# Queries of batches 1 to 3 from high and low parts of weights and rows, in three single-pass products

## The chip, the cores and the metric

The kernel runs on one core of a Trainium2 chip. The metric is the time of one execution on the device in microseconds, as the median of several runs. One execution was also taken with the hardware profiler; its rows are what the prediction reads.

## The reference, cut to what matters

The reference is one layer of a gated cross-attention block with a mixture of experts behind it, for 4 batches of 512 rows of 512 numbers. Only the first step matters here:

```
q = layernorm(x) @ w_q.T        # 4 x 512 x 512, 32 heads of 16
k = ctx @ w_k.T                 # 8 groups of 16
v = ctx @ w_v.T
scores = q k^T / 4, causal, masked; softmax; times v; out @ w_o.T + b_o
x = x + tanh(g_xattn) * that    # then the experts on layernorm(x)
```

Queries and keys are wanted in float32 accuracy, since the scores feed an exponential.

## The kernel before, in words

The program is a chain of stages with a barrier between two of them: `stage_project`, `stage_attend`, `stage_close`, `stage_shared`, `stage_experts`. The change lies in `stage_project` (line 242), which lasts from 0 to about 115 us. It goes through four batches, one block of code per engine, and the engines meet by semaphores.

TensorE (lines 455 to 527): for batch b it turns the four 128-row chunks of the normalised rows (`turn`, line 474, four 128x128 transposes each into one of two PSUM banks `tps`), with the keys of the batch (`keys`, line 458) behind the second turn and the values (`values`, line 466) behind the fourth. In batch 0 keys and values stand first. Then come the queries (`queries`, line 493): four output groups i of 128 query columns, each into its own PSUM bank `proj[i]` and each made of four products, over the four 128-row slices k of the weights `wq`, against the turned rows `xnT` of 512 columns. Both are float32, and the profiler records two instructions for each such product. In the last batch `scores` (line 483) puts one pair of score products of the first two rounds behind each of the sixteen query products. A pair goes into two of three banks, and `max_pair` (line 201) first waits until VectorE has taken the maxima of the pair before: all but the last of them, or, for one pair in a round of eight, all of them (line 204). One transpose of the maxima (`turn_maxima`, line 214) follows the tenth pair.

ScalarE (lines 410 to 453) copies PSUM to SBUF in this order per batch: two turned chunks, the keys' high part, two more turned chunks, the values, the root for the next batch's layernorm (`deviation`), and then the high part of each query group as it comes. A high part is the copy in the type float32r, which holds fewer bits and goes through TensorE in a single pass; the low part is what is left, PSUM minus high part.

VectorE (lines 368 to 408) makes the low part of the keys, then the layernorm of the next batch (`normalise`), then the low parts of the four query groups; in the last batch also the maxima of the score pairs, four pairs ahead of each low part.

GpSimd (lines 321 to 366) fills constants and then stores the keys' parts of each batch to DRAM. SP issues all loads, then the stores of the queries' parts in order of the batches (`store_q`, line 284), and behind those of batch 1 the loads of the first three rounds of scores (line 317).

The buffers `parts[0]` and `parts[1]` hold the high and low parts of a batch in turns; batch 0 and 2 use the first, 1 and 3 the second. Fillers of TensorE (48 bf16 products, line 527) close the stage.

For comparison, `stage_shared` (line 1438) and `stage_experts` (line 1729) already multiply in three float32r products, high by high, high by low and low by high.

Of the kernel before, what the change touches and what calls it, by code (L numbers as in the profile page):

```python
# [16 lines left out]
P = 128  # L17
# [78 lines left out]
def begin(eng, *made):  # L96

    for sem in made:
        eng.sem_inc(sem, 1)  # L99
# [142 lines left out]
def stage_project(nc, io, dram):  # L242

    SPIN, SEAM = 48, 48
    with ExitStack() as c:  # L245
# [2 lines left out]
        sem = dsem = lambda n: c.enter_context(nc.semaphore(n))  # L248

        parts = [sb(f"p_parts{i}", [P, KD + 1, 2, SEQ], F32R) for i in range(2)]  # L250
        wq, wk, wv = sb("wq", [P, KD, D]), sb("wk", [P, KD, P]), sb("wv", [P, KD, P])
        x, ctx = [residual(io, b) for b in range(BATCH)], [context(io, b) for b in range(BATCH)]
        xn, xnT = sb("p_xn", [P, CH, D]), sb("p_xnT", [P, KD, SEQ])
        stats, mv, rstd = sb("p_stats", [P, CH, 6]), sb("p_mv", [P, CH, 2]), sb("p_rstd", [P, CH])
        root, work, eps = sb("p_root", [P, CH]), sb("p_work", [P, CH]), sb("p_eps", [P, 1])
        v = io["v_all"]
        ident = io["ident"]
        padi, padb = sb("p_padi", [BATCH, SEQ], I32), sb("p_padb", [BATCH, SEQ], F32R)
        padf = sb("p_padf", [BATCH, SEQ])
# [8 lines left out]
        s_kmm, s_vmm, s_qmm = sem("p_skmm"), sem("p_svmm"), sem("p_sqmm")  # L268
        s_khi, s_klo, s_qhi, s_qlo, s_vcp = (sem(f"p_s{n}") for n in ("khi", "klo", "qhi", "qlo", "vcp"))
        s_fill, s_mask, s_warm = (sem(f"p_s{n}") for n in ("fill", "mask", "warm"))  # L270
        s_one = dsem("p_sone")
        s_pad, s_padb, s_padf, s_pout = dsem("p_spad"), sem("p_spadb"), sem("p_spadf"), dsem("p_spout")
        s_qout, s_kout = io["s_qout"], io["s_kout"]
# [2 lines left out]
        @block.sync  # L276
        def _(eng):
            def load_ctx(b):
                eng.dma_start(ctx[b], io["ctxT"][:, b * SEQ:(b + 1) * SEQ].rearrange("(c p) n -> p c n", p=P)).then_inc(s_ctx[b], 16)

            def load_x(b):
                eng.dma_start(x[b], io["x"][b * SEQ:(b + 1) * SEQ, :].rearrange("(j p) d -> p j d", p=P)).then_inc(s_x[b], 16)

            def store_q(b):
                for i in range(KD):
                    at = dram["q"][b * GROUPS + 2 * i:b * GROUPS + 2 * i + 2].rearrange("g t r s j n -> s (g t r) (j n)")
                    eng.wait_ge(s_qhi, b * KD + i + 2)
# [9 lines left out]
            eng.dma_start(padi[:], io["mask"]).then_inc(s_pad, 16)  # L297
            load_x(0)
            eng.dma_start(wv[:], io["wvT"].rearrange("(c p) n -> p c n", p=P)).then_inc(s_wv, 16)
            eng.dma_start(wq[:], io["wqT"].rearrange("(c p) n -> p c n", p=P)).then_inc(s_wq, 16)  # L300
            for b in range(1, BATCH):
                load_x(b)
                load_ctx(b)
            eng.wait_ge(s_padb, 2)
            for b in range(BATCH):
                eng.dma_start(dram["k"][b * GROUPS:(b + 1) * GROUPS, ROW_PAD].rearrange("(o g) n -> o g n", o=1),
                              padb[b:b + 1, :].bitcast(F32).rearrange("p (o n) -> p o n", o=1).broadcast_to([1, GROUPS, SEQ])).then_inc(s_pout, 16)
            for b in range(BATCH):
                store_q(b)
                if b == 1:  # L310
                    eng.wait_ge(s_pout, 16 * BATCH)
                    eng.wait_ge(s_one, 64 * NB)
                    eng.wait_ge(s_qout[0], 16 * 2 * KD)
                    eng.wait_ge(s_kout[0], 48)
                    eng.wait_ge(s_vcp, 2)
                    for i in range(NB - 1):
                        load_scores(eng, io, dram, i, i)
                    for i in range(NB - 1):
                        load_values(eng, io, i, i)

        @block.gpsimd
        def _(eng):
            begin(eng, s_eps, s_ones, s_fill, s_mask, s_warm)
            eng.memset(io["onesb"], 1.0).then_inc(s_warm, 1)
            eng.memset(io["before"], 1.0).then_inc(s_fill, 1)
            eng.memset(io["ident"], 0.0).then_inc(s_fill, 1)
# [32 lines left out]
                    eng.dma_start(k[r][HALF * t + ROW_MAX:HALF * t + ROW_MAX + 1].bitcast(F32), const[:, 1]).then_inc(s_one, 16)  # L359
            for b in range(BATCH):  # L360
                at = dram["k"][b * GROUPS:(b + 1) * GROUPS]
                eng.wait_ge(s_khi, b + 2)
                for slot in range(2):
                    eng.dma_start(at[:, slot:2 * HD:2], parts[b % 2][:, KD, 0].bitcast(F32)).then_inc(s_kout[b % 2], 16)
                eng.wait_ge(s_klo, b + 2)
                eng.dma_start(at[:, 2 * HD:3 * HD], parts[b % 2][:, KD, 1].bitcast(F32)).then_inc(s_kout[b % 2], 16)

        @block.vector
        def _(eng):
            begin(eng, s_newton, s_st, s_mv, s_xn, s_klo, s_qlo, s_padb, s_padf, io["s_rmax"], io["s_mr"])  # L370
            def normalise(b):
                eng.wait_ge(s_x[b], 16)
                for j in range(CH):
# [12 lines left out]
            eng.tensor_copy(padf[:], padi[:]).then_inc(s_padf, 1)  # L386
            eng.wait_ge(s_padf, 2)
            eng.tensor_scalar(padb[:], padf[:], 0.0, NEG, ALU.is_equal, ALU.mult).then_inc(s_padb, 1)
            def low_keys(b):
                eng.wait_ge(s_khi, b + 2)  # L390
                part = parts[b % 2][:, KD]
                eng.tensor_tensor(part[:, 1, :], proj[KD][:], part[:, 0, :].bitcast(F32), ALU.subtract).then_inc(s_klo, 1)

            normalise(0)
            for b in range(BATCH):
                low_keys(b)
                if b + 1 < BATCH:
                    normalise(b + 1)
                for i in range(KD):
                    if b == BATCH - 1:  # L400
                        for n in range(i * KD, (i + 1) * KD):
                            round, turn, j = n // (2 * CH), n // 2 % CH, n % 2
                            maxima(eng, io, round, round, turn, j)
                            if n == 2 * CH + 1:
                                take_row(eng, io, 0, 0)
                    part = parts[b % 2][:, i]
                    eng.wait_ge(s_qhi, b * KD + i + 2)
                    eng.tensor_tensor(part[:, 1, :], proj[i][:], part[:, 0, :].bitcast(F32), ALU.subtract).then_inc(s_qlo, 1)

        @block.scalar  # L410
        def _(eng):
            begin(eng, s_root, s_xT, s_khi, s_qhi, s_vcp)
            def deviation(b):
                eng.wait_ge(s_mv, (b + 1) * CH + 1)
                eng.activation(root[:], mv[:, :, 1], ACT.Sqrt, bias=eps[:]).then_inc(s_root, 1)

            def take_turned(b, j):
                eng.wait_ge(s_tr, b * CH + j + 2)
                eng.activation(xnT[:, :, j * P:(j + 1) * P], tps[j % 2], ACT.Copy).then_inc(s_xT, 1)

            def take_keys(b):
                eng.wait_ge(s_kmm, b + 2)
                if b >= 2:
                    eng.wait_ge(s_kout[b % 2], 48)
# [10 lines left out]
            for b in range(BATCH):  # L435
# [20 lines left out]
        def _(eng):  # L456
# [36 lines left out]
            def queries(b):  # L493
                eng.wait_ge(s_xT, (b + 1) * CH + 1)
                if b:
                    eng.wait_ge(s_qlo, b * KD + 1)
                for i in range(KD):
                    for k in range(KD):
                        mm = eng.matmul(proj[i][:], wq[:, k, i * P:(i + 1) * P], xnT[:, k, :], start=k == 0, stop=k == KD - 1)
                        if k == KD - 1:  # L500
# [1354 lines left out]
```

## Time and profile before

| | |
|---|---|
| runs | 1211.01 us median of 3 (1208.92 to 1211.45) |
| the profiled execution | 1205.16 us |
| its span, first to last instruction | 1203.4 us |
| mean granted TensorE clock | 0.990 of full speed |
| busy: TensorE, VectorE, ScalarE, GpSimd | 1163.3, 614.1, 563.9, 650.2 us |

The profiled execution is 5.85 us shorter than the runs' median and 1.76 us longer than its span. A granted clock of 1.00 is 2.4 GHz. PE is TensorE, PEld its weight loads, DVE is VectorE, ACT is ScalarE, POOL is GpSimd, SP issues transfers. `Lnnn` is a line of the kernel. Busy time of PE is modelled: its records of one float32 product overlap, so distances between starts say more than durations.

### The profile page before, as it was taken

Reading aid. Unit: us, or ns where it says so; the run is one execution under the profiler, and the core shown is the slowest. Engines: PE = TensorE matmul, PEld = TensorE weight load, DVE = VectorE, ACT = ScalarE, POOL = GpSimd, SP = SyncE. Lnnn points to the kernel's source line nnn. Section 1 sums busy time; section 2 is a strip of 40 time slices with the busy share of each in tenths; the row PEclk is TensorE's granted clock in tenths of the full one; section 3 lists DMA queues with packets and bytes.
Section 4 is the critical chain, followed back from the end, with each engine's and each line's share of the span. In section 5 each row is a group of like instructions: output and inputs, shape, how many; then the busy total and the mean of one; then the engine's idle time right before and its main releaser. Section 6 shows DMA issues by size and latency. Waiting matters only on the chain. (4 is left out here: it accounts for less than half of the span.)

```text
span 1203.4 us, 23285 instructions
## 1 busy us (share of the span) xinstructions
PE 1163.3 (97%) x7651; PEld 899.5 (75%) x7652; DVE 614.1 (51%) x1785; ACT 563.9 (47%) x981; POOL 650.2 (54%) x697
## 2 busy tenths in 40 slices
PE   7999999999997989999998999999999999999996
PEld 5564555555543468888877999999999999999995
DVE  5337999999966958721344033333423444442100
ACT  2221777777751333323222554554554554554552
POOL 5010333334342615788863666666767666676663
PEclk9999999999998999999998999999999999999998
DMA  9462544444449350120313655666666666566443
GB/s 347 176 189 96 156 128 127 127 126 130 133 143 238 137 213 33 38 65 12 138 56 116 144 118 110 143 150 149 142 150 150 144 150 148 144 150 149 74 69 42
DMA packets 77309, 157.95 MB, mean 131 GB/s; under 512 B 12933, under 2 KB 18821, under 8 KB 76217
## 3 DMA queue, kind: packets, MB, share of 16 engines
q1 hardware_dynamic: 54152, 107.12, 27.7%
q0 software_dynamic: 23088, 49.94, 21.7%
q8 instruction: 40, 0.66, 0.2%
q14 instruction: 29, 0.23, 0.1%
HBM read 101.97 MB, written 52.64 MB: 128 GB/s over the span
## 5 line engine op out<-in xcount | busy, mean ns | idle before, releaser
L1589 DVE CAST e_w<-e_w 128x480 fp32r<-128x480 f32 x135 | 80.5, 596 | 300.7 <-DMA e_w<-in_w2T 296.5
L670 DVE CUSTOM_DVE_ANT_0 a_mb<-a_mb,late 128x512 f32<-128x512 f32 (+1 forms) x480 | 217.4, 530 | 6.2 <-PE a_mb L714 4.6
L1750 PE MATMUL e_yps<-e_w,e_hT 128*128 x711 | 190.3, 394 | 0.9 <-ACT e_hT L1656 0.9
L576 POOL TENSOR_SCALAR_AFFINE_SELECT a_at<-a_at 128x256 f32<-128x256 f32 (+1 forms) x192 | 94.2, 491 | 171.0 <-ACT a_at L656 170.9
L656 ACT ACTIVATE a_at<-a_eb 128x1024 f32<-128x1024 f32 (+1 forms) x192 | 163.5, 870 | 38.3 <-PE a_eb L735 25.8
L1729 PE MATMUL e_up<-e_w,e_xT 128*128 x948 | 170.5, 329 | 0.0
L1729 PE MATMUL e_gate<-e_w,e_xT 128*128 x948 | 167.8, 326 | 0.5 <-issue 0.5
L1616 POOL DMA_INDIRECT out<-e_y,scatter x79 | 128.3, 1624 | 69.0 <-ACT e_y L1665 59.7
L1729 PEld LDWEIGHTS e_gate<-e_w,e_xT 128*128 128x128 f32 x948 | 158.8, 191 | 7.6 <-issue 0.9
L1750 PEld LDWEIGHTS e_yps<-e_w,e_hT 128*128 128x128 f32 x711 | 131.7, 189 | 25.6 <-issue 1.2
L1729 PEld LDWEIGHTS e_up<-e_w,e_xT 128*128 128x128 f32 x948 | 149.9, 189 | 0.0
L714 PE MATMUL a_mb<-a_k,a_q 49*128 49x512 f32 (+1 forms) x480 | 132.6, 373 | 0.8 <-PEq L245 0.8
L714 PEld LDWEIGHTS a_mb<-a_k,a_q 49*128 49x128 f32 x480 | 74.3, 184 | 65.6 <-DVE a_mx L670 39.3
L1634 POOL TENSOR_TENSOR e_h<-e_act,e_upc 128x352 f32<-128x352 f32 x79 | 76.8, 972 | 70.0 <-ACT e_upc L1678 69.9
L1621 POOL TENSOR_TENSOR e_hT<-e_hc,e_hT 128x384 fp32r<-128x384 f32 x78 | 87.0, 1115 | 41.0 <-ACT e_hc L1658 40.9
L758 PE MATMUL a_pv<-a_at,a_v 128*32 128x128 f32 (+1 forms) x1792 | 102.3, 327 | 0.5 <-POOL a_at L576 0.4
L1596 DVE TENSOR_TENSOR e_w<-e_w 128x480 fp32r<-128x480 f32 x135 | 96.8, 717 | 4.7
L1652 ACT ACTIVATE e_xT<-e_xps 128x512 fp32r<-128x512 f32 x79 | 47.2, 597 | 90.3 <-PE e_xps L1720 90.3
L105 POOL DMA_INDIRECT e_x<-dx,gather x79 | 80.7, 1021 | 13.8 <-issue 3.7
L735 PE MATMUL a_eb<-a_q,a_k 50*128 50x512 f32 (+1 forms) x256 | 84.2, 420 | 0.1
L1672 ACT ACTIVATE e_act<-e_gate 128x352 f32<-128x352 f32 x79 | 36.7, 465 | 93.0 <-PE e_gate L1729 93.0
L1387 POOL DMA_INDIRECT dtable<-r_put,r_place x64 | 66.2, 1034 | 17.3 <-issue 17.3
(256 smaller groups left out, 1783.1 us busy)
## 6 DMA issues: line engine op xcount, KB each, us to landing
e_w<-in_w13T SPq DMA_DIRECT2D x16, 1408.0 KB
dq<-p_parts SPq DMA_DIRECT2D x32, 256.0 KB, 2.4
a_q<-dq SPq DMA_DIRECT2D x64, 128.0 KB
do<-a_o SPq DMA_DIRECT2D x32, 256.0 KB, 2.3
e_w<-in_w2T SPq DMA_DIRECT2D x16, 512.0 KB
a_k<-dk SPq DMA_DIRECT2D x64, 98.0 KB
e_w<-in_ctxT SPq DMA_DIRECT2D x4, 1024.0 KB, 15.2
e_w<-in_x SPq DMA_DIRECT2D x4, 1024.0 KB, 13.6
```

The lines of the kernel that those rows point to most:

```text
L105: eng.indirect_dma_start(out=io["rows"][n], out_offset=None, in_=dram["x2"], in_offset=bass.IndirectOffsetOnAxis(ap=io["gather"][:, g:g + ...
L576: eng.affine_select(out=square, in_=square, compare_op=ALU.is_ge, fill=0.0, base=0, pattern=[[0, 2 * len(js)], [1, P]], channel_multiplier ...
L656: eng.activation(to, scores, ACT.Exp, scale=0.25).then_inc(s_exp, 1)
L670: eng.tensor_tensor_reduce(out=b[:, 0:w], in0=b[:, 0:w], in1=io["late"][:, SEQ - w:SEQ], scale=1.0, scalar=3 * NEG, op0=ALU.add, op1=ALU.m ...
L714: mm = eng.matmul(b, q[r][rows, j, ch * P:(ch + 1) * P], k[r][rows, 0:b.shape[-1]], start=True, stop=True)
L735: return eng.matmul(eb[u % 2][:, t, n0:SEQ], keys, q[r][rows, js[0], n0:SEQ], start=True, stop=True)
L758: mm = eng.matmul(pv[32 * h:32 * h + 32, cols], v[of % NB][:, ch, :], at[of % 2][:, ch, 2 * j + t, cols], start=ch == 0 and n0 == 0, stop= ...
L1596: eng.tensor_tensor(w[rows, r, rest], w[rows, r, rest].bitcast(F32), w[rows, r, cols].bitcast(F32), ALU.subtract).then_inc(s_low, 1)
L1616: eng.indirect_dma_start(out=out, out_offset=bass.IndirectOffsetOnAxis(ap=io["scatter"][:, g:g + 1], axis=0), in_=y[n][:], in_offset=None, ...
L1621: eng.tensor_tensor(hT[r][:, 1], hc[:], hT[r][:, 0].bitcast(F32), ALU.subtract).then_inc(s_hlow, 1)
L1729: mm = eng.matmul(out[r][:], xT[r][:, mine, k, :], w[:, bass.ds(buf, 1), its * SIDE + at:its * SIDE + at + INTER].rearrange("p b n -> p (b ...
L1750: mm = eng.matmul(yps[:], hT[r][0:size, mine, n, :], w[0:size, bass.ds(buf, 1), its * SIDE + at:its * SIDE + at + D].rearrange("p b n -> p ...
```

## The change

Batch 0 stays as it is, in float32; only its turned rows go into another buffer (`first`). For batches 1 to 3 each query group becomes twelve float32r products instead of four float32 ones: high weights by high rows, low weights by high rows, high weights by low rows. The high rows are ScalarE's copy as before, now in float32r. The low rows are four new VectorE subtractions per batch (`low_turned`), two ahead of the low keys and two behind them. The high weights are one new ScalarE copy in batch 0, and the low weights four new GpSimd subtractions ahead of batch 1's key stores. A turn into a bank now waits for the low rows made from it, and the queries of batches 1 to 3 wait for the low rows of their batch and for the low weights. In the last batch a score pair stands behind every third product, which makes sixteen as before. To make room, the float32 weights and batch 0's turned rows lie in the second parts buffer, and the mask's rows too; ScalarE's take of batch 1's keys therefore waits until the mask's rows are stored.

```diff
-        wq, wk, wv = sb("wq", [P, KD, D]), sb("wk", [P, KD, P]), sb("wv", [P, KD, P])
+        wlow, wk, wv = sb("p_wlow", [P, KD, D], F32R), sb("wk", [P, KD, P]), sb("wv", [P, KD, P])
+        wq, first = parts[1][:, KD // 2:KD].bitcast(F32).rearrange(...), parts[1][:, 0:KD // 2].bitcast(F32).rearrange(...)
-        xn, xnT = sb("p_xn", [P, CH, D]), sb("p_xnT", [P, KD, SEQ])
+        xn, xnT = sb("p_xn", [P, CH, D]), sb("p_xnT", [P, KD, SEQ], F32R)
+        xlow, whigh = sb("p_xlow", [P, KD, SEQ], F32R), sb("p_whigh", [P, KD, D], F32R)
-        padi, padb = sb("p_padi", [BATCH, SEQ], I32), sb("p_padb", [BATCH, SEQ], F32R)
-        padf = sb("p_padf", [BATCH, SEQ])
+        padi, padf, padb = xn[0:BATCH, 0].bitcast(I32), parts[1][0:BATCH, KD, 0].bitcast(F32), parts[1][0:BATCH, KD, 1]
...
 # GpSimd, in front of the stores of a batch's keys
+                if b == 1:
+                    eng.wait_ge(s_whigh, 2)
+                    eng.wait_ge(s_qmm, KD + 1)
+                    for k in range(KD):
+                        eng.tensor_tensor(wlow[:, k], wq[:, k], whigh[:, k].bitcast(F32), ALU.subtract).then_inc(s_wlow, 1)
...
 # VectorE
+            def low_turned(b, j):
+                columns = slice(j * P, (j + 1) * P)
+                eng.wait_ge(s_xT, b * CH + j + 2)
+                eng.tensor_tensor(xlow[:, :, columns], tps[j % 2], xnT[:, :, columns].bitcast(F32), ALU.subtract).then_inc(s_xlow, 1)
...
+                if b:
+                    low_turned(b, 0)
+                    low_turned(b, 1)
                 low_keys(b)
+                if b:
+                    low_turned(b, 2)
+                    low_turned(b, 3)
...
 # ScalarE
-                eng.activation(xnT[:, :, j * P:(j + 1) * P], tps[j % 2], ACT.Copy).then_inc(s_xT, 1)
+                eng.activation((xnT if b else first)[:, :, j * P:(j + 1) * P], tps[j % 2], ACT.Copy).then_inc(s_xT, 1)
...
+                if b == 1:
+                    eng.wait_ge(s_pout, 16 * BATCH)
                 eng.activation(parts[b % 2][:, KD, 0, :], proj[KD][:], ACT.Copy).then_inc(s_khi, 1)
...
+                if b == 0:
+                    eng.wait_ge(s_wq, 16)
+                    eng.activation(whigh[:], wq, ACT.Copy).then_inc(s_whigh, 1)
...
 # TensorE, in turn(b, j)
+                if t >= CH + 2:
+                    eng.wait_ge(s_xlow, t - CH)
 # and in queries(b)
+                if b:
+                    eng.wait_ge(s_whigh, 2)
+                    eng.wait_ge(s_wlow, KD + 1)
+                    eng.wait_ge(s_xlow, b * CH + 1)
                 for i in range(KD):
-                    for k in range(KD):
-                        mm = eng.matmul(proj[i][:], wq[:, k, i * P:(i + 1) * P], xnT[:, k, :], start=k == 0, stop=k == KD - 1)
...
+                    for n, (weights, rows, k) in enumerate((weights, rows, k) for weights, rows in ((whigh, xnT), (wlow, xnT), (whigh, xlow)) for k in range(KD)):
+                        mm = eng.matmul(proj[i][:], weights[:, k, columns], rows[:, k, :], start=n == 0, stop=n == 3 * KD - 1)
+                        if n == 3 * KD - 1:
                             mm.then_inc(s_qmm, 1)
-                        if b == BATCH - 1:
-                            scores(i * KD + k)
+                        if b == BATCH - 1 and n % 3 == 2:
+                            scores(i * KD + n // 3)
```

## Rows read from the trace of the kernel before

**Rows 1.** The page, busy time, share of the span, instructions.
```profile
PE 1163.3 (97%) x7651; PEld 899.5 (75%) x7652; DVE 614.1 (51%) x1785; ACT 563.9 (47%) x981; POOL 650.2 (54%) x697
```
**Rows 2.** Windows: stretch, length, busy (count) per engine, PEclk, DMA share, GB/s.
```profile
0.00:112.00 112.00, 104.77 (x433) 57.29 (x434) 55.95 (x198) 24.02 (x45) 23.23 (x47) 1.00 0.61 207
```
**Rows 3.** Timeline of TensorE, batch 1: start, duration, line, operation, count.
```profile
35.57 3.60 PE L463 MATMUL p_proj<-e_w,wk 128*128 128x512 f32 x8
39.00 1.04 PE L480 MATMUL a_mb<-ident,p_xn 128*128 128x128 f32 x8
...
43.45 13.90 PE L499 MATMUL p_proj<-p_xnT,wq 128*128 128x512 f32 x32
57.18 1.04 PE L480 MATMUL a_mb<-ident,p_xn 128*128 128x128 f32 x8
```
**Rows 4.** TensorE's timeline in the shared expert, and its loads by line (min/median/max ns).
```profile
498.98 2.88 PE L1438 MATMUL s_up<-s_xT,s_ws 128*128 x12
501.70 1.52 PE L1438 MATMUL s_gate<-s_xT,s_ws 128*128 x6
...
L1438 PEld LDWEIGHTS s_gate<-s_xT,s_ws x288: 186/188/189, 447.3 to 612.2; 128*128 128x128 f32 x144
```
**Rows 5.** Timeline of TensorE, batch 3: score pairs (L210) and query products.
```profile
90.87 0.49 PE L210 MATMUL a_mb<-a_k,a_q 49*128 49x256 f32 x2
91.29 1.12 PE L499 MATMUL p_proj<-p_xnT,wq 128*128 128x512 f32 x2
92.35 0.44 PE L210 MATMUL a_mb<-a_k,a_q 49*128 49x256 f32 x2
...
93.77 0.45 PE L210 MATMUL a_mb<-a_k,a_q 49*128 49x256 f32 x2
```
**Rows 6.** Timeline of VectorE, batch 3, a pair's maxima; in brackets idle time and releaser.
```profile
91.28 0.30 DVE L225 CUSTOM_DVE_ANT_0 a_mb<-a_mb,late 128x128 f32<-128x128 f32 x1 [0.47 <-PE a_mb L210]
...
92.15 0.14 DVE L225 DVE_READ_ACCUMULATOR2_ANT a_mx<- 128x1 f32 x1
```
**Rows 7.** Timeline of all engines at the end of the stage.
```profile
112.96 0.69 DVE L408 TENSOR_TENSOR p_parts<-p_proj,p_parts 128x512 fp32r<-128x512 f32 x1
...
115.58 0.33 SPq L175 DMA_DIRECT2D a_q<-dq  x1
```
**Rows 8.** Groups by form, ScalarE, 0 to 130 us: busy, mean ns, idle before.
```profile
L656 ACT ACTIVATE a_at<-a_eb 128x1024 f32<-128x1024 f32 x5 | 5.0, 1014 | 2.4 <-PE a_eb L734 1.3 <-PE a_eb L735 1.1
```
**Rows 9.** Timeline of ScalarE, batches 0 and 1.
```profile
22.29 0.30 ACT L415 ACTIVATE p_root<-p_mv,p_eps 128x4 f32<-128x4 f32 x1 [1.55 <-DVE p_mv L377]
24.59 0.60 ACT L453 ACTIVATE p_parts<-p_proj 128x512 fp32r<-128x512 f32 x1 [2.00 <-PE p_proj L499]
...
39.20 0.60 ACT L425 ACTIVATE p_parts<-p_proj 128x512 fp32r<-128x512 f32 x1 [2.73 <-PE p_proj L463]
```
**Rows 10.** One line's instructions, GpSimd in the experts: min/median/max ns.
```profile
L1621 POOL TENSOR_TENSOR e_hT<-e_hc,e_hT x78: 1002/1011/1571, 652.4 to 1186.4; 128x384 fp32r<-128x384 f32 x78
```
**Rows 11.** Timeline of GpSimd, the key stores of batch 1.
```profile
40.09 1.19 POOL L364 DMA_DIRECT2D dk<-p_parts  x2 [19.73 <-ACT p_parts L425]
```
**Rows 12.** Groups by form, VectorE, 0 to 113 us.
```profile
L408 DVE TENSOR_TENSOR p_parts<-p_proj,p_parts 128x512 fp32r<-128x512 f32 x16 | 11.0, 689 | 21.1 <-ACT p_parts L453 21.1
```
**Rows 13.** Timeline of VectorE, around batch 1.
```profile
35.52 0.69 DVE L408 TENSOR_TENSOR p_parts<-p_proj,p_parts 128x512 fp32r<-128x512 f32 x1 [2.74 <-ACT p_parts L453]
39.83 0.69 DVE L392 TENSOR_TENSOR p_parts<-p_proj,p_parts 128x512 fp32r<-128x512 f32 x1 [3.62 <-ACT p_parts L425]
...
48.71 0.68 DVE L408 TENSOR_TENSOR p_parts<-p_proj,p_parts 128x512 fp32r<-128x512 f32 x1
```
**Rows 14.** Windows, one microsecond, all engines.
```profile
39.00:40.00 1.00, 1.00 (x11) 1.00 (x10) 0.17 (x1) 0.80 (x2) 0.00 (x0) 1.00 0.00 0
```
**Rows 15.** Windows before and in a stretch of low granted clock.
```profile
636.00:639.00 3.00, 0.00 (x0) 0.00 (x0) 0.00 (x0) 0.00 (x0) 0.18 (x2) 1.00 0.16 61
...
642.00:645.00 3.00, 3.00 (x11) 3.00 (x11) 0.00 (x0) 0.00 (x0) 0.00 (x0) 0.50 1.04 403
```

More of the change, by code:

```diff
@@ L250, in stage_project @@
         parts = [sb(f"p_parts{i}", [P, KD + 1, 2, SEQ], F32R) for i in range(2)]
-        wq, wk, wv = sb("wq", [P, KD, D]), sb("wk", [P, KD, P]), sb("wv", [P, KD, P])
+        wlow, wk, wv = sb("p_wlow", [P, KD, D], F32R), sb("wk", [P, KD, P]), sb("wv", [P, KD, P])
+        wq, first = parts[1][:, KD // 2:KD].bitcast(F32).rearrange("p i t n -> p (i t) n"), parts[1][:, 0:KD // 2].bitcast(F32).rearrange("p i t n -> p (i t) n")
         x, ctx = [residual(io, b) for b in range(BATCH)], [context(io, b) for b in range(BATCH)]
-        xn, xnT = sb("p_xn", [P, CH, D]), sb("p_xnT", [P, KD, SEQ])
+        xn, xnT = sb("p_xn", [P, CH, D]), sb("p_xnT", [P, KD, SEQ], F32R)
+        xlow, whigh = sb("p_xlow", [P, KD, SEQ], F32R), sb("p_whigh", [P, KD, D], F32R)
         stats, mv, rstd = sb("p_stats", [P, CH, 6]), sb("p_mv", [P, CH, 2]), sb("p_rstd", [P, CH])
@@ L270, in stage_project @@
         s_fill, s_mask, s_warm = (sem(f"p_s{n}") for n in ("fill", "mask", "warm"))
+        s_xlow, s_whigh, s_wlow = sem("p_sxlow"), sem("p_swhigh"), sem("p_swlow")
         s_one = dsem("p_sone")
@@ L296, in _ @@
             load_ctx(0)
-            eng.dma_start(padi[:], io["mask"]).then_inc(s_pad, 16)
+            eng.dma_start(padi, io["mask"]).then_inc(s_pad, 16)
             load_x(0)
             eng.dma_start(wv[:], io["wvT"].rearrange("(c p) n -> p c n", p=P)).then_inc(s_wv, 16)
-            eng.dma_start(wq[:], io["wqT"].rearrange("(c p) n -> p c n", p=P)).then_inc(s_wq, 16)
+            eng.dma_start(wq, io["wqT"].rearrange("(c p) n -> p c n", p=P)).then_inc(s_wq, 16)
             for b in range(1, BATCH):
@@ L322, in _ @@
         def _(eng):
-            begin(eng, s_eps, s_ones, s_fill, s_mask, s_warm)
+            begin(eng, s_eps, s_ones, s_fill, s_mask, s_warm, s_wlow)
             eng.memset(io["onesb"], 1.0).then_inc(s_warm, 1)
@@ L369, in _ @@
         def _(eng):
-            begin(eng, s_newton, s_st, s_mv, s_xn, s_klo, s_qlo, s_padb, s_padf, io["s_rmax"], io["s_mr"])
+            begin(eng, s_newton, s_st, s_mv, s_xn, s_klo, s_qlo, s_padb, s_padf, s_xlow, io["s_rmax"], io["s_mr"])
             def normalise(b):
@@ L385, in _ @@
             eng.wait_ge(s_pad, 16)
-            eng.tensor_copy(padf[:], padi[:]).then_inc(s_padf, 1)
+            eng.tensor_copy(padf, padi).then_inc(s_padf, 1)
             eng.wait_ge(s_padf, 2)
-            eng.tensor_scalar(padb[:], padf[:], 0.0, NEG, ALU.is_equal, ALU.mult).then_inc(s_padb, 1)
+            eng.tensor_scalar(padb, padf, 0.0, NEG, ALU.is_equal, ALU.mult).then_inc(s_padb, 1)
             def low_keys(b):
@@ L411, in _ @@
         def _(eng):
-            begin(eng, s_root, s_xT, s_khi, s_qhi, s_vcp)
+            begin(eng, s_root, s_xT, s_khi, s_qhi, s_vcp, s_whigh)
             def deviation(b):
@@ L496, in queries @@
                     eng.wait_ge(s_qlo, b * KD + 1)
+                if b:
+                    eng.wait_ge(s_whigh, 2)
+                    eng.wait_ge(s_wlow, KD + 1)
+                    eng.wait_ge(s_xlow, b * CH + 1)
                 for i in range(KD):
-                    for k in range(KD):
-                        mm = eng.matmul(proj[i][:], wq[:, k, i * P:(i + 1) * P], xnT[:, k, :], start=k == 0, stop=k == KD - 1)
-                        if k == KD - 1:
+                    columns = slice(i * P, (i + 1) * P)
+                    if b == 0:
+                        for k in range(KD):
+                            mm = eng.matmul(proj[i][:], wq[:, k, columns], first[:, k, :], start=k == 0, stop=k == KD - 1)
+                        mm.then_inc(s_qmm, 1)
+                        continue
+                    for n, (weights, rows, k) in enumerate((weights, rows, k) for weights, rows in ((whigh, xnT), (wlow, xnT), (whigh, xlow)) for k in range(KD)):
+                        mm = eng.matmul(proj[i][:], weights[:, k, columns], rows[:, k, :], start=n == 0, stop=n == 3 * KD - 1)
+                        if n == 3 * KD - 1:
                             mm.then_inc(s_qmm, 1)
-                        if b == BATCH - 1:
-                            scores(i * KD + k)
+                        if b == BATCH - 1 and n % 3 == 2:
+                            scores(i * KD + n // 3)
             eng.wait_ge(s_warm, 3)
```

## The prediction

> **What bounds the kernel now.** I read the page first: TensorE is busy for 97% of the span [rows 1]. The page's chain of waits lies in the last half of the span, where the change does nothing, so I cut the span at 112 us, where the projections end. There TensorE is busy 104.77 of 112 us at a granted clock of 1.00, 2.4 GHz, VectorE 55.95 [rows 2]. The timeline of TensorE then shows no idle time between its pieces in batch 1: two turns and the keys, two turns and the values, then the queries, 32 records from 43.45 to 57.18 us, where batch 2's first turn starts [rows 3]. Batch 2 repeats the pattern. So a microsecond less of query products there is a microsecond less of the span, as long as no operand is late. Batch 3 is different: its query products stand between pairs of score products, and VectorE has to clear the banks of these [rows 5].
>
> **The products of batches 1 and 2.** They go from 16 float32 products to 48 float32r ones per batch. A float32 product is two records, 13.73 / 32 = 0.429 us apart, 0.858 us in all [rows 3]. Float32r products of the same form, 128x128 weights against 512 columns, run in the shared expert: a group of 12 from 498.98 to 501.70 us, 0.2267 us each [rows 4]. The price of a new batch is 48 x 0.2267 = 10.88 us, and 13.73 - 10.88 = 2.85 us are saved, 5.70 in two batches. The ends of this price: the float32 records at half their distance, 0.2145 us (10.30, saving 3.43), and the rival of exposed loads below.
>
> The Trainium skill (TensorE: Matmul & The Clock Gate, Back-to-back issue gap) gives an isolated product N/2.4 + 2.5 ns, 215.7 ns for 512 columns. By it a batch would take 10.35 us, and the whole change would give some 1.6 us more; the row above is slower, and I go by it.
>
> **Batch 3.** From one score pair to the next is 1.48 us (90.87 to 92.35) or 1.42 (92.35 to 93.77) [rows 5]. In the first of these the pair takes 0.42 us until a query product starts (91.29). That product's two records take 1.06 us, up to 92.35, where two in the stream take 0.858. I read the 0.20 as two weight loads of 0.10 that aren't hidden where pairs of 49 rows and products of 128 rows follow each other [rows 5]. With three float32r products between pairs 1.06 us becomes 3 x 0.227 + 2 x 0.10 = 0.88, and 0.18 us are saved per pair, at 1.30 and 1.25 us. Can VectorE keep that? It takes 0.87 us for a pair (91.28 to the second read at 92.15 [rows 6]) and 0.69 for the low part behind each fourth pair: 4 x 0.87 + 0.69 = 4.2 us against 4 x 1.28 = 5.1. It can. But one pair in eight (the third of a round) waits for both maxima of the pair before, and these end 92.15 + 0.14 - 90.87 = 1.42 us after that pair began, where TensorE would be there after 1.30; with the semaphore I take 1.47, so 0.17 is lost in the first round. In the second the turn of the maxima stands there and covers it. The first pair waits for ScalarE's copy of the values and gains 0.09 only. Sum: 15 x 0.178 + 0.09 - 0.17 = 2.6 us. Bounds: 0, if the pairs keep their pace, and 16 x 0.18 = 2.9. I take 2.6, since in the rows VectorE idles 0.47 us before a pair, waiting for TensorE [rows 6].
>
> The end of the stage stays as it is: behind the last pair come two maxima, the low part at 112.96, its store, and the next stage's first transfer at 115.58 [rows 7].
>
> **What is added, and what hides it.**
> The high weights, one ScalarE copy of 2048 columns: at 1014 ns for 1024 [rows 8] at most 2.03 us. It stands behind the root of 22.29 to 22.59 and ends by 24.6; the next ScalarE work began at 24.59 [rows 9]. Should it be late, only batch 0's first high part moves, and the next is due 3.4 us later. Cost 0.
>
> The low weights, four GpSimd subtractions of 512 columns. They wait for batch 0's last query product, whose low part VectorE made at 35.52 [rows 13], say for 35 us, and must be done before batch 1's queries at 43.45 [rows 3]. The nearest row is 1.011 us for 384 columns, 1.571 at its longest [rows 10]; by columns 1.35, at most 2.1. So 5.4 us, to 40.4; at the longest 8.4 us, to 43.4. Both are in time: cost 0, and beyond 2.1 us each, four times the excess. Behind them on GpSimd stand the stores of batch 1's keys, issued at 40.09 until now [rows 11]; they move by about 1 us. Their readers are SP's loads of scores of later rounds and the reuse of the buffer in batch 3, 40 us on.
>
> The low turned rows, four VectorE subtractions per batch of 0.69 us, the price of the like row [rows 12]. Two come before the low keys, while TensorE makes keys (35.57 to 39.00): the low part at 35.52 goes first [rows 13], then 36.2 to 37.6, and the turn at 39.00 that now needs the first of them has 2 us to spare. Two follow the low keys at 39.83 and end near 41.9, before the queries at 43.45. The normalising behind them starts 1.4 us later; its end, where batch 1's first low part starts at 48.71 [rows 13], becomes 50.1, and batch 2's turns need it at 43.45 + 10.88 = 54.3. Cost 0, with 1.5 us of cover; were that gone, a late microsecond would cost one in each of three batches.
>
> The mask's rows lie in the second parts buffer now, so ScalarE's take of batch 1's keys at 39.20 waits for their stores. Between 39 and 40 us no DMA moved anything [rows 9, 14], so they had landed. Cost 0. SP keeps its order; its stores follow the high and low parts, and the loads of scores behind batch 1's stores go out earlier with them.
>
> **Sum.** 5.7 + 2.6 = 8.3 us. What follows is started by semaphores and moves as a whole. The profiled execution is 1205.16 us for a span of 1203.4 and would be 1196.9. The runs' median, 1211.01, lies 5.9 above the profiled one, a difference of executions; the same 8.3 off it gives 1202.7.
>
> **Rivals.**
> *Weight loads show, and it is slower.* A batch loads 48 sets of weights where it loaded 32, in the same rows of the array. If each product showed the 0.10 us that batch 3's changes show, it would cost 0.327, a batch 15.7 us, 2.0 more than before, and batch 3's three products and pair load 1.08 for 1.06. In all 4 us slower, 1215. It decides from 13.73 / 48 = 0.286 us per product on. Against it: in the shared expert a load of 0.188 us stands behind each product and the distance is still 0.227 [rows 4]; for it, only batch 3, where the shapes alternate. The chance is 5%; a compiled form that isn't single-pass would end here too, another 1%.
> The Trainium skill (TensorE: Matmul & The Clock Gate, Part 3, The mechanism) says that a weight load overlaps running products only where the row group differs, and so speaks for this rival. This trace disagrees in [rows 4].
>
> *Batch 3 keeps its pace.* The pairs stay at 1.45 us because the banks' waits set them. Then 5.7 us are saved: 1205.3. For it: a wait on the maxima is at every pair. Against it: VectorE's idle time. 17%.
>
> *The low weights are late.* GpSimd at 3 us each would end at 47, 3.5 us late: 4.8 saved, 1206.2. At 4.2 each the gain is gone. Against it: the longest row. 8%.
>
> *The clock takes it back.* Behind stretches where TensorE stood the granted clock falls to 0.50, 1.2 GHz, for some microseconds: it did nothing from 636 to 639 us and runs at half speed from 642 to 645 [rows 15]. A program that arrives 8 us earlier can meet other stretches; three microseconds at half speed cost 1.5, so one longer or shorter stretch changes the time by 1 to 3 us. This and the scatter of runs could leave a change under 2.4 us: 7%, around 1210.
>
> **How the numbers follow.** My forecast has 62%, by itself 1199 to 1206 (8.3, with the ends of the prices and 2 us of clock and scatter). What a measurement can tell from no change is 0.2%, 2.4 us. Faster: the forecast, batch 3's pace and the late low weights, 62 + 17 + 8 = 87%. Same 7%, slower 6%. The range for 8 in 10 takes in the forecast and the second rival and some of the others: 1198 to 1208.5.
>
> **What would show it.** TensorE's query group of batches 1 and 2 at 10.9 us, 0.227 each; batch 3's pairs 1.25 to 1.30 apart; no TensorE idle time named GpSimd or the low rows in front of the queries; the next stage's first transfer at 107.3 instead of 115.58. I am wrong if the products are 0.28 us apart or more, if the queries of batch 1 start after 44 us, if pairs stay at 1.45, or if the stages behind 116 us lose what was won.

## The result, and the profile after

| | before | after |
|---|---|---|
| median of five runs each, side by side | 1211.01 us | 1203.23 us |
| their range | 1208.06 to 1212.92 | 1201.84 to 1206.71 |
| the profiled execution, its span, its mean granted clock | 1205.16, 1203.4, 0.990 | 1206.71, 1204.9, 0.981 |
| next stage's first transfer | 115.58 us [rows 7] | 111.18 us |

The ratio of the times is 0.995, its 95% interval 0.9932 to 0.9969, which is 3.8 to 8.2 us of 1211: the kernel became faster. The medians lie 7.8 us apart, where 8.3 were worked out. The two profiled executions alone would have told the opposite (1205.16 before, 1206.71 after), so the comparison of the traces has to be made by stage.

Batch 1 on TensorE's timeline of the kernel after (start, duration, line, operation, count; L505 turns, L486 keys, L494 values, L530 batch 0's queries, L534 the others). The rows answer to [rows 3]:

```profile
22.09 16.40 PE L530 MATMUL p_proj<-p_parts 128*128 128x512 f32 x32 [0.78 <-ACT p_parts L437]
38.33 1.04 PE L505 MATMUL a_mb<-ident,p_xn 128*128 128x128 f32 x8
...
43.51 3.74 PE L494 MATMUL a_mb<-wv,e_w 128*128 128x128 f32 x32
47.01 1.17 PE L534 MATMUL p_proj<-p_xnT,p_whigh 128*128 128x512 f32 x4
48.02 1.08 PE L534 MATMUL p_proj<-p_xnT,p_wlow 128*128 128x512 f32 x4
...
56.19 1.07 PE L534 MATMUL p_proj<-p_xnT,p_wlow 128*128 128x512 f32 x4
57.10 1.08 PE L534 MATMUL p_proj<-p_xlow,p_whigh 128*128 128x512 f32 x4
58.01 1.04 PE L505 MATMUL a_mb<-ident,p_xn 128*128 128x128 f32 x8
...
77.68 1.04 PE L505 MATMUL a_mb<-ident,p_xn 128*128 128x128 f32 x8
```

Batch 1's queries last from 47.01 to 58.01, 11.00 us for 13.73. A group of four products takes 0.907 us (56.19 to 57.10 is 0.91), 0.227 each, and only the first group is 0.1 us longer. No bracket with idle time stands before 47.01: no operand was late. From turn to turn (58.01 to 77.68) batch 2 now takes 19.67 us; before it took 22.50 (57.18 [rows 3] to 79.68). Rows of the kernel before, against which this and what follows are read:

```profile
34.69 1.04 PE L480 MATMUL a_mb<-ident,p_xn 128*128 128x128 f32 x8
...
79.68 1.04 PE L480 MATMUL a_mb<-ident,p_xn 128*128 128x128 f32 x8
...
89.39 0.49 PE L210 MATMUL a_mb<-a_k,a_q 49*128 49x256 f32 x2
...
111.68 0.44 PE L210 MATMUL a_mb<-a_k,a_q 49*128 49x256 f32 x2
```

The first row of the kernel after shows what hid the gain in this profile: batch 0's queries, which the change leaves in float32, are 16.40 us long, for 13.97 before. Windows of TensorE (busy time, PEclk, DMA share, GB/s) in the kernel after:

```profile
16.00:18.00 2.00, 0.49 (x3) 0.69 1.06 374
18.00:20.00 2.00, 2.00 (x10) 0.50 1.07 377
...
24.00:26.00 2.00, 2.00 (x4) 0.50 1.04 402
26.00:28.00 2.00, 2.00 (x4) 0.75 1.04 398
```

and of the kernel before (all five engines, then PEclk):

```profile
16.00:18.00 2.00, 0.42 (x4) 0.45 (x5) 1.93 (x11) 0.00 (x0) 2.00 (x4) 1.00 1.07 376
18.00:20.00 2.00, 1.66 (x14) 1.24 (x12) 2.00 (x5) 1.44 (x3) 1.25 (x3) 1.00 1.07 378
```

TensorE stands for about 3 us before batch 0's turns in both. In this execution of the kernel after the clock fell to 0.50 behind that gap, in this one of the kernel before it didn't. So I count from the end of batch 0's queries to the next stage's first transfer: 115.58 - 34.69 = 80.89 us before (batch 1's first turn started at 34.69), 111.18 - 38.33 = 72.85 after. That is 8.04 us. Counted between these two events the other profiles agree, whatever their clock in batch 0: 80.89 us in both further profiles of the kernel before, 72.85 to 72.90 in all five of the kernel after, with and without the fillers that come below.

Batch 3's score pairs (L210) in the kernel after, which answer to [rows 5], and the end of the stage, which answers to [rows 7]:

```profile
87.28 0.50 PE L210 MATMUL a_mb<-a_k,a_q 49*128 49x256 f32 x2
...
88.59 0.49 PE L210 MATMUL a_mb<-a_k,a_q 49*128 49x256 f32 x2
...
90.07 0.44 PE L210 MATMUL a_mb<-a_k,a_q 49*128 49x256 f32 x2
...
91.34 0.44 PE L210 MATMUL a_mb<-a_k,a_q 49*128 49x256 f32 x2
...
107.28 0.44 PE L210 MATMUL a_mb<-a_k,a_q 49*128 49x256 f32 x2
...
108.57 0.68 DVE L426 TENSOR_TENSOR p_parts<-p_proj,p_parts 128x512 fp32r<-128x512 f32 x1
...
111.18 0.32 SPq L175 DMA_DIRECT2D a_q<-dq  x1
```

The distances are 1.31, 1.48 and 1.27 us; the second is the pair that waits for both maxima. From the first pair to the last it is 20.00 us (87.28 to 107.28), and 22.29 before (89.39 to 111.68).

The added work in the kernel after, one row each from the timelines of ScalarE, GpSimd and VectorE:

```profile
22.44 1.89 ACT L471 ACTIVATE p_whigh<-p_parts 128x2048 fp32r<-128x2048 f32 x1
```

```profile
38.65 4.96 POOL L368 TENSOR_TENSOR p_wlow<-p_parts,p_whigh 128x512 fp32r<-128x512 f32 x4 [18.35 <-PE p_proj L530]
```

```profile
39.77 1.28 DVE L404 TENSOR_TENSOR p_xlow<-a_mb,p_xnT 128x512 fp32r<-128x512 f32 x2
```

The low weights end at 43.61, 3.4 us before the queries of batch 1. The low rows are two at a time here, one alone takes 0.68 us; the last two of batch 1 end at 45.36, 1.65 us before the queries.

### The profile page after: what moved, and what is told of

Same layout as the page of the kernel before. It is cut to its first block and busy times, and to the rows that moved or that the text cites. A ratio compares the mean times of both kernels' runs of the same rounds, so it can differ in the third digit from the quotient of the medians.

```text
span 1204.9 us, 23404 instructions
## 1 busy us (share of the span) xinstructions
PE 1164.2 (97%) x7699; PEld 914.8 (76%) x7700; DVE 618.5 (51%) x1797; ACT 566.1 (47%) x982; POOL 651.2 (54%) x701
```

## The experiments

The theory: each product costs 0.227 us of TensorE, the added work lies beside it, and the span follows the stage. The rivals: the change shifts how much of the program runs at the low clock; the added work is nearly late; batch 3 is limited by something other than its products.

### Both kernels again, and both with fillers

The first two are the kernels before and after, unchanged. In the other two bf16 products without use fill three places where TensorE stands: 44 in batch 0 before the first turn, 90 in `stage_close`, 30 before the experts. The edit is the same in both kernels; of the three places the first is shown:

```diff
+            for _ in range(44):
+                eng.matmul(tps[0][:, 0, :], io["onesb"], io["before"], start=True, stop=True)
```

> The kernel before, unchanged, for its clock in several executions. Theory A (the products save 8.0 us in the first stage, and where the granted clock falls is a scatter of its own): its mean granted clock scatters as widely as the changed kernel's (0.981 to 0.986), between 0.980 and 0.990, and its times lie some 8 us above those of the changed kernel at the same clock. Theory B (the change itself brings more low clock, which eats a part of its gain): the clock of before is at 0.988 or more in every execution, and at equal clock the gap would be 10 us or more.

> The changed kernel, unchanged. Both theories: 7 to 9 us faster than before in the median. Theory A: the query group of batch 0 takes 13.8 us unless the clock falls there, as it did in the first profile (22.09 to 38.33 us); the stage ends at 107.5 us when it doesn't. Theory B: the clock falls in batch 0 every time, and the stage ends near 111 us again.

> The changed kernel with bf16 fillers on TensorE where it stands idle and the clock falls behind it: 44 ahead of batch 0's first turn, 90 in the closing stage ahead of batch 1's projection, 30 at the start of the experts' stage. Theory A: the clock no longer falls in these places, mean clock 0.989 or more, 3 to 6 us faster than the changed kernel (6.8 us at half speed cost up to 3.4 each), and the spread of its times is smaller. Rival: the fillers end after the data they wait for has come, and the time is the same or some us longer.

> The same fillers in the kernel before. Theory A: 3 to 6 us faster than before, and 8.0 us slower than the changed kernel with fillers, since clock and products add up. Theory B: the gap between the two filled kernels is 10 us or more, because the changed kernel has lost more to the clock than before has.

| | median, range | ratio to before (95%) | next stage's first transfer |
|---|---|---|---|
| before again | 1209.69, 1203.42 to 1210.92 | 0.9992 (0.9976 to 1.0008) | 116.44 us |
| after again | 1203.62, 1197.66 to 1205.43 | 0.9948 (0.9924 to 0.9971) | 108.65 us |
| after, filled | 1199.65, 1198.24 to 1200.44 | 0.9918 (0.9897 to 0.9939) | 107.36 us |
| before, filled | 1208.0, 1201.22 to 1212.49 | 0.998 (0.9963 to 0.9997) | 115.43 us |

In the unfilled pair both profiles have a stretch of low clock in batch 0 (0.83 from 16 to 26 us in each), and the next stage starts 7.79 us earlier; batch 0 ended 0.24 us later there, so from the end of batch 0 it is 80.89 - 72.86 = 8.03 us. In the filled pair neither has one, and the next stage starts 8.07 us earlier (8.01 from the end of batch 0), between SP's rows of the kernel after

```profile
107.36 0.32 SPq L175 DMA_DIRECT2D a_q<-dq  x1
```

and of the kernel before

```profile
115.43 0.32 SPq L175 DMA_DIRECT2D a_q<-dq  x1
```

The scatter goes with the clock: over 115 executions of the unfilled kernels (before, after and the next three below, each kernel with a level of its own) the time falls with the mean granted clock, 9.9 +- 0.8 us for 0.01 (correlation -0.91 in 83 executions of the kernel before, -0.95 in 14 of the kernel after). The mean clock is the same in both, 0.9851 and 0.9846, so the rival that the change brings more low clock falls. At equal clock the kernel after is 7.1 +- 0.6 us faster, the stage shows 8.0. That up to 1 us is given back behind the stage, I could not show, and it stays open: from the next stage's first transfer to the end of the span the three profiles of the kernel before last 1087.8, 1092.0 and 1095.2 us, those of the kernel after 1093.7, 1087.9 and 1091.3, a scatter wider than what is looked for.

The filled medians lie 8.35 us apart, but not by the change alone. The fillers ahead of the experts ran too long, and not alike in the two kernels: from the bf16 products that close the shared stage to the experts' first turn it is 6.85 us with them and 5.35 without in the kernel after, 8.33 and 5.32 in the kernel before. The kernel after gained 4.0 us by all the fillers, the kernel before only 1.7, where 3 to 6 were expected of each. So the fillers before the experts are left out below.

### Four products instead of three

The loop line is cut to its list of products; the pairs of batch 3 now stand behind every fourth product.

```diff
-for weights, rows in ((whigh, xnT), (wlow, xnT), (whigh, xlow))
+for weights, rows in ((whigh, xnT), (wlow, xnT), (whigh, xlow), (wlow, xlow))
```

> A fourth single-pass product is added, low weights by low rows, so a batch has 64 products. Theory A (in batches 1 and 2 the price is the count of products times 0.227 us, with weight loads hidden): a batch's queries take 64 x 0.2267 = 14.5 us, 0.8 more than the float32 form's 13.73; in batch 3 a score pair comes every 1.50 us; the stage ends 10 to 11 us later than the changed kernel's, and the time is 2 to 3 us above before. Rival C (float32r products are cheaper for another reason than their count, such as shorter waits at the groups' ends, and the saving of some us stays): still 3 us or more below before.

1212.31 us (1207.39 to 1216.13), ratio to before 1.0017 (0.9998 to 1.0035). On TensorE's timeline batch 1's queries last from 45.99 to 60.62:

```profile
45.99 1.17 PE L534 MATMUL p_proj<-p_xnT,p_whigh 128*128 128x512 f32 x4
...
59.71 1.07 PE L534 MATMUL p_proj<-p_xlow,p_wlow 128*128 128x512 f32 x4
60.62 1.03 PE L505 MATMUL a_mb<-ident,p_xn 128*128 128x128 f32 x8
```

14.63 us is 3.63 more than with three, just 16 x 0.227. Batch 3's pairs come 1.50 to 1.56 us apart (93.71, 95.27, 96.81, 98.31), 0.23 more. From the end of batch 0's queries to the next stage's first transfer (37.32 to 120.92) it is 83.60 us, 10.75 more than 72.85, for 48 products more, which are 48 x 0.2267 = 10.88. At equal clock the time is 9.6 +- 0.8 us above the kernel after, again about 1 us less than the stage says. Against the kernel before the interval takes in no change, so the runs alone don't tell 2 us slower from the same. The products carry the time one for one in the stage: 64 of 0.227 us are no cheaper than 32 float32 records of 0.429, and with 48 the change gains.

### The low weights made twice

```diff
+                    eng.wait_ge(s_wlow, KD + 1)
+                    for k in range(KD):
+                        eng.tensor_tensor(wlow[:, k], wq[:, k], whigh[:, k].bitcast(F32), ALU.subtract).then_inc(s_wlow, 1)
```

The queries wait for the second making.

> GpSimd makes the four low weights twice, 10.0 us instead of 4.96. Theory A (they are hidden, with a cover of 3 to 4 us): they end 10.0 us after batch 0's last query product, batch 1's queries start 1.5 to 2 us late with TensorE idle ahead of them, and the time is that much above the changed kernel's. Rival D (GpSimd's work is hidden by more than that, or the queries' start is set by something else): batch 1's queries start at once after the values, and nothing is lost.

1202.49 us (1198.70 to 1203.97), ratio 0.9926 (0.9903 to 0.995). TensorE's timeline shows the wait, once:

```profile
47.86 1.17 PE L537 MATMUL p_proj<-p_xnT,p_whigh 128*128 128x512 f32 x4 [1.65 <-POOL p_wlow L371]
```

5.04 us more of GpSimd's work (its second four start at 42.65, the first at 37.61) cost 1.65 us of idle time, so 3.4 us of it were covered, as the first profile says. Rival D falls. At equal clock the time is 0.7 +- 1.1 us above the kernel after: in the runs 1.65 us can't be told from nothing.

### One product: what limits when TensorE doesn't

Only high weights by high rows; the low-weight and low-row products are left out, while their operands are still made. The loop line is again cut to its list of products.

```diff
-for weights, rows in ((whigh, xnT), (wlow, xnT), (whigh, xlow))
+for weights, rows in ((whigh, xnT),)
```

> Leaves out the products with low weights and with low rows: 16 products per batch in batches 1 to 3. Theory A: the queries take 16 x 0.227 = 3.6 us; then VectorE is late next, since its work for a batch (normalising 7.7, nine subtractions at 0.6) is 13.1 us where TensorE needs 12.4, so TensorE waits about 1 us for the normalised rows ahead of the first turn of batches 2 and 3. In batch 3 the pairs come at VectorE's pace, 1.05 to 1.1 us. The stage ends about 15 us earlier than the changed kernel's, at 92 to 93 us with the clock up in batch 0. Rival E (batch 3's pairs can't go faster than 1.25 us, a fixed delay from score product to maximum and back sets them): batch 3 keeps 20 us from the first to the last pair.

1190.81 us (1189.26 to 1194.61), ratio 0.9849 (0.9826 to 0.9871). VectorE becomes late for the turns of batches 2 and 3, by 0.64 and 0.38 us; here batch 2:

```profile
44.28 3.88 PE L534 MATMUL p_proj<-p_xnT,p_whigh 128*128 128x512 f32 x16
48.81 1.11 PE L505 MATMUL a_mb<-ident,p_xn 128*128 128x128 f32 x8 [0.64 <-DVE p_xn L389]
```

So with three products it is TensorE and not VectorE that sets the pace of these batches. In batch 3 the pairs first came 0.85 us apart (72.03, 72.88), then 1.52 for the third, which waits for both maxima, and 0.96 (74.40, 75.36): no fixed delay holds them at 1.25. Then the clock fell. The timeline and the windows of this kernel:

```profile
72.03 0.49 PE L210 MATMUL a_mb<-a_k,a_q 49*128 49x256 f32 x2 [0.46 <-ACT a_vall L450]
72.88 0.50 PE L210 MATMUL a_mb<-a_k,a_q 49*128 49x256 f32 x2
74.40 0.44 PE L210 MATMUL a_mb<-a_k,a_q 49*128 49x256 f32 x2 [0.58 <-DVE a_mx L225]
75.36 0.69 PE L210 MATMUL a_mb<-a_k,a_q 49*128 49x256 f32 x2
76.70 0.79 PE L210 MATMUL a_mb<-a_k,a_q 49*128 49x256 f32 x2
```

```profile
74.00:76.00 2.00, 1.51 (x6) 0.68 (x6) 1.37 (x7) 0.60 (x1) 0.00 (x0) 0.81 1.03 384
76.00:78.00 2.00, 2.00 (x5) 0.83 (x4) 2.00 (x8) 0.00 (x0) 0.00 (x0) 0.50 0.93 352
```

At half clock the ordinary pairs came every 1.34 to 1.45 us, slower than with three products at full clock. From the first pair to the last it was 20.37 us (72.03 to 92.40). That is rival E's sign, but its cause is the clock and not a fixed delay. The clock was low in all four executions of this kernel (0.974 to 0.979 on average). So the expectation missed: from the end of batch 0's queries to the next stage's first transfer (35.60 to 97.82) it is 62.22 us, 10.6 less than with three products, where 15 were expected. What batch 3's bound without the clock is, this run leaves open.

### Two fillers, none before the experts

The kernel after with the 44 fillers in batch 0 and 120 in the close stage, run on two occasions.

> The changed kernel with the fillers ahead of batch 0's first turn (44) and 120 of them in the closing stage, none in the experts' stage, where the first filled version began its first turn 1.5 us late (6.85 us after the stage before instead of 5.34). Theory A: 1 to 2 us below the first filled version, 1197 to 1199 us, with the clock falling in the experts' start as before. Rival: the fillers in the experts' stage had won more by the clock than they cost, and this version is 1 to 3 us slower than the first filled one.

> The kernel after with 44 and 120 filler products (stages project and close) once more, on the same chip as the next run, as its base. Theory (one hundredth of mean granted clock is about 9.7 us): the same as the first time, about 1197 us, ratio 0.989 to 0.991, mean granted clock about 0.992; in the trace no half clock in batch 0 or in the close stage, and the next stage's first transfer near 107.5 us. If the first time had been luck of the clock and not the fillers, it falls back to 1202 to 1203 us at a clock of 0.985.

1196.92 us (1195.86 to 1200.53), ratio 0.9899 (0.988 to 0.9918), and 1199.76 us (1195.33 to 1202.37), ratio 0.9923 (0.9903 to 0.9943). The first profile's windows show the close stage's stretch of low clock gone (PEclk 0.83 there in the kernel after):

```profile
360.00:380.00 20.00, 20.00 (x154) 12.64 (x153) 16.25 (x35) 4.24 (x3) 4.58 (x3) 1.00 0.92 261
```

The second occasion was 2.8 us slower than expected. Its profile has full clock in batch 0 too, but 0.74 from 425 to 440 us and 0.81 from 440 to 455, in gaps that the fillers don't touch. Against the first filled version (1199.65) one occasion is 2.7 us faster and the other the same, so what the fillers before the experts cost or gain stays open.

### Batch 0 in three products too

On the kernel with two fillers. The high weights are made before batch 0's turns, the low weights straight behind; in batch 0 all high-by-high products come first, the low weights last. Two cuts of the edit; the new wait stands under `if t >= 2`:

```diff
+                order = [(i, p) for p in range(3) for i in range(KD)] if b == 0 else [(i, p) for i in range(KD) for p in range(3)]
...
-                if t >= CH + 2:
-                    eng.wait_ge(s_xlow, t - CH)
+                    eng.wait_ge(s_xlow, t)
```

> Base is the kernel after with the 44 and 120 fillers; batch 0's queries too are made in three products of parts (high weights by ScalarE before the first turned tile, low weights by GpSimd straight behind, low rows by VectorE; within batch 0 all high-by-high products first, the low weights last). Theory A (0.227 us for each product, added work beside): batch 0's group takes 48 x 0.2267 = 10.9 instead of 14.0 us, -3.1; the third and fourth turned tile now wait for the low rows of the first two (0.64 us each on VectorE behind the row's own work), +0.7 to +1.3; sum about -2.1, next stage's first transfer near 105.4 and a time of about 1195 us. Rival B (the added work of batch 0 is exposed): low weights can begin on GpSimd only behind its transfer issues at 17.8 us and end at about 22.8, needed at about 29, so there is room; if they are late, TensorE shows idle time released by GpSimd inside batch 0's group, 1 to 3 us, and the time is 1196 to 1198. Rival C (VectorE, with 2.6 us more ahead of batch 1's rows, is what batch 1's turned tiles then wait for): idle before batch 1's first transpose released by VectorE's rows, and the gain is gone: 1197.

1204.4 us (1196.17 to 1211.04), ratio 0.997 (0.9952 to 0.9987): slower than its base of the same occasion. Batch 0 on TensorE's timeline (L503 turns, L532 queries):

```profile
20.26 1.23 PE L503 MATMUL a_mb<-ident,p_xn 128*128 128x128 f32 x8 [1.64 <-DVE p_xlow L403]
22.22 5.42 PE L532 MATMUL p_proj<-p_xnT,p_whigh 128*128 128x512 f32 x16 [0.73 <-issue]
27.48 3.79 PE L532 MATMUL p_proj<-p_xlow,p_whigh 128*128 128x512 f32 x16
31.10 3.80 PE L532 MATMUL p_proj<-p_xnT,p_wlow 128*128 128x512 f32 x16
34.73 1.04 PE L503 MATMUL a_mb<-ident,p_xn 128*128 128x128 f32 x8
```

The expectation missed the price of the wait. The third turn waits 1.64 us for the low rows of the first (0.7 to 1.3 were expected). About 1 us of it, as I estimate, comes from VectorE's four row operations just ahead, which took 2.90 us here and 1.91 elsewhere. The clock then falls (0.51 from 22 to 24 us, 0.64 from 24 to 26), and the first 16 products take 5.26 us (22.22 to 27.48) for 3.63. Batch 1 starts at 34.73, no earlier than with float32 in batch 0 (34.82 in the base's profile). Neither rival showed: the low weights were in time, and batch 1's turn waited for nothing. This profile is the fastest of the twelve executions; most others had a mean clock of 0.984 or less (the base 0.988 to 0.991), and why, their missing traces don't say. So that this wait makes the median slower is likely and not shown.

### The same, with the wait taken away

Two things are changed together: the third and fourth turned tiles of batch 0 go into two projection banks that are still free, and GpSimd makes the low weights only when VectorE has made the rows (the added `s_xn` wait). Three cuts of the edit:

```diff
+        turned = lambda b, j: tps[j % 2] if b or j < 2 else proj[j][:].rearrange("p (c n) -> p c n", c=CH)
...
+                    eng.wait_ge(s_xn, CH + 1)
...
-                if t >= 2:
+                if b:
```

> As the last kernel (all four batches in three products, 44 and 120 fillers), with what held batch 0 back there taken away: its third and fourth turned tiles go into two projection banks that are still free, so no transpose waits for VectorE's low rows (there 1.64 us idle before the third tile, then the granted clock at 0.51 to 0.64 from 22 to 26 us and 5.42 instead of 3.63 us for the first 16 products), and GpSimd begins the low weights only when VectorE has made batch 0's rows (beside them the four rows took 2.90 instead of 1.91 us). Theory A (0.227 us a product; what batch 0 lost was the wait and the clock behind it): first query product near 20.3 us, group 10.9 us, batch 1's first transpose near 31.3 instead of 34.7 us, next stage's first transfer near 104.4; time 1194 to 1197 us, mean granted clock 0.988 to 0.992. Rival B (three products in batch 0 bring the low clock by themselves, or exposed work of another engine keeps the group at 12 us and more): no gain over the kernel with two fillers alone, 1199 to 1204 us at a clock of 0.984, and the profile shows half clock in or behind batch 0 although no transpose waited.

1195.08 us (1192.12 to 1198.58), ratio 0.9883 (0.9862 to 0.9905), the lowest median of the versions that make all three products:

```profile
20.23 3.91 PE L536 MATMUL p_proj<-p_xnT,p_whigh 128*128 128x512 f32 x16 [0.89 <-issue]
23.98 3.79 PE L536 MATMUL p_proj<-p_xlow,p_whigh 128*128 128x512 f32 x16
27.61 3.79 PE L536 MATMUL p_proj<-p_xnT,p_wlow 128*128 128x512 f32 x16
31.24 1.03 PE L505 MATMUL a_mb<-ident,p_xn 128*128 128x128 f32 x8
```

Batch 0's queries take 11.01 us, batch 1 starts at 31.24, and the next stage's first transfer goes out at 104.12, where 31.3 and 104.4 were expected. With the wait the low clock in batch 0 went too: PEclk is 1.00 from 14 to 28 us, and all six executions have a mean clock of 0.987 to 0.991. Which of the two edits did it, this run doesn't separate. The next stage starts 3.2 and 3.6 us earlier than in the two profiles of the kernel with two fillers (107.31 and 107.72). The medians lie 1.8 and 4.7 us lower, on another occasion, and the intervals of the ratios overlap: in the runs the last step is not clear of noise.

## Why the prediction was right, point by point

- **Batches 1 and 2**: predicted 10.88 us and -2.85 each; measured 11.00 for batch 1's queries and, from turn to turn, 22.49 - 19.68 = 2.81 in batch 1 and 22.50 - 19.67 = 2.83 in batch 2. The price per product from the shared expert held to a thousandth of a microsecond; the missing 0.1 us is the first group, 1.01 us long.
- **Batch 3**: predicted -2.6; measured 8.04 - 2.81 - 2.83 = 2.4, of which 22.29 - 20.00 = 2.29 from the first pair to the last. The ordinary pairs lie 1.26 to 1.33 us apart (1.30 and 1.25 predicted), the third pair comes after 1.48 (1.47). This is the term that was too large, by 0.2 us: an ordinary pair saves 0.164 us and not 0.178 (without the third pair, 22.29 - 1.48 and 20.00 - 1.48 over 14 distances). Some 0.10 us at each change between a pair and the products is there before and after; that a weight load makes it, as the prediction read it, no run shows.
- **Added work at nothing**: right, with the sizes of the high weights 1.89 us (at most 2.03), the low weights 1.24 each (1.35) and the low rows 0.68 (0.69). The doubled low weights measured their cover, 3.4 us; the low rows had 1.65 us (1.5 predicted).
- **Sum**: 8.3 predicted for the stage, 8.04 from the end of batch 0 in the first pair of profiles, 8.03 and 8.01 in the two others. That the medians of the first result came so near, 7.8, is in part luck of the scatter: on the second occasion they lie 6.1 apart. The next stage's first transfer was not at 107.3 in the profile after but at 111.18, by the low clock in batch 0, 3.64 us; with that filled it was at 107.36.
- **Weight loads**: they did not show in batches 1 and 2. In the kernel after each of the 144 products has a load with a median of 0.188 us, and the distance stays 0.227. The rule of the Trainium skill (TensorE: Matmul & The Clock Gate, Part 3, The mechanism) that spoke for this rival does not describe these rows: the loads lie beside running products of the same rows of the array. The same section also names a background weight buffer as a way to load early; whether that is what happens here, no run shows.
- **Batch 3's pace and late low weights**: both rivals fell, by the pairs' distances and by the missing idle time.
- **The clock**: the mean clock of the two kernels is the same, so on average it takes nothing back that these runs can tell. But the executions of one kernel lie up to 10 us apart with it (1202.95 to 1213.21 before), more than the change. The prediction gave it "1 to 3 us"; the profile after lost 3.64 in batch 0 alone.

## What to carry to other kernels

Where TensorE's timeline has no gap, three float32r products of 0.227 us in place of a float32 product of two records of 0.429 save 0.18 us, and a fourth product eats that up. The price is best read from another stage that already does it. Before the change is extended, look for the new waits of the operands: in batch 0 a wait of 1.64 us and the low clock behind it used up what the products won, in the one profile taken, and with two spare banks and a later start of GpSimd both were gone. With a clock that moves, compare kernels by stages between the same two events, and not by the spans of two profiles.

## What the runs showed of the hardware that was not expected

- The granted clock falls to half behind gaps of about 3 us before batch 0's turns in some executions and not in others of the same kernel (before: none in the first profile, 0.83 from 16 to 26 us in the second).
- Waits far shorter can precede it: 0.58 us between two pairs of the one-product kernel, 1.64 and 0.73 us in batch 0 of the kernel with all four batches. So in batch 3 a kernel with less to do per pair (one product, 1.34 to 1.45 us) was slower there than one with three (1.26 to 1.33).
- Products that compute nothing made the kernel faster: with 164 of them the medians were 1196.9 and 1199.8 us, for 1203.2 and 1203.6 without. The first is clear of noise (ratio to before at most 0.9918, without them at least 0.9924 on its second occasion), the second is not.
- VectorE's row operation and GpSimd's subtraction were slower side by side, in the one profile that has them so. In the first kernel with all four batches one of VectorE's four row operations of batch 0 took 1.49 us, where the median of the line is 0.54, while GpSimd made the low weights (1.27 to 1.44 us each):

```profile
L388 DVE TENSOR_SCALAR p_xn<-e_w,p_mv,p_rstd x16: 533/542/1486, 16.6 to 68.4; 128x512 f32<-128x512 f32 x16
```

  With GpSimd starting behind the rows the longest is 0.546, and the low weights take 1.27 to 1.30:

```profile
L390 DVE TENSOR_SCALAR p_xn<-e_w,p_mv,p_rstd x16: 537/541/546, 16.7 to 64.9; 128x512 f32<-128x512 f32 x16
```

  VectorE's low rows, which read PSUM, ran beside GpSimd's subtraction in both kernels and stayed at 0.67 to 0.69 us each.
